# Attention in half-blocks of queries, ten hidden tiles in the first FFN, and the rows of the maxima sent from ScalarE's queue

## What is computed

```
x = x + attn(ln(x))      # 16 heads of 16, rotary, causal softmax over 1024 keys, output matrix Wo
x = x + ffn(ln(x))       # down(silu(gate(x)) * up(x)), hidden 768, weights int / 127
x = x + wkv(ln(x))       # RWKV-6 time mixing: five mixed inputs, decays, scan with a 64x64 state per head
x = x + ffn(ln(x))       # the same weights
```

## Time and profile before

| | |
|---|---|
| median of 3 runs | 3494.27 us (3494.21 to 3497.56) |
| the profiled execution | 3494.36 us, of which the span from first to last instruction is 3492.6 |
| busy share of the span | PE 86%, VectorE 71%, ScalarE 37%, GpSimd 39% |
| mean granted TensorE clock | 0.943 of 2.4 GHz |
| one batch in the middle | 422 to 424 us from one batch's first maxima to the next's |

### The profile page before, as it was taken

How to read it: one execution, slowest core, us unless ns; L and a number is a source line. 1 busy time by engine, 2 the same in 40 slices (tenths; PEclk the granted TensorE clock), 3 DMA queues, 4 the chain that set the end, 5 groups by cost and what they waited for, 6 DMA issues and landing times.

```text
span 3492.6 us, 47078 instructions
## 1 busy us (share of the span) xinstructions
PE 3005.8 (86%) x17056; PEld 1832.7 (52%) x17056; DVE 2492.0 (71%) x5105; ACT 1308.3 (37%) x2721; POOL 1351.1 (39%) x1276
## 2 busy tenths in 40 slices
PE   2488988889888888889888898889988889898898
PEld 1236565365643666335663457535565355753667
DVE  4575787667875687857878568785687857877566
ACT  0264323632346322453225532265313643136322
POOL 0123561245612365124551346313462134622455
PEclk9699998999989999899998999999998999989999
DMA  3600024000330005100150002400024000240000
GB/s 129 111 2 13 19 37 81 2 13 19 59 59 2 13 19 79 39 14 10 22 92 15 14 10 43 83 2 13 15 40 81 2 14 19 37 80 2 1 1 13
DMA packets 68888, 115.04 MB, mean 33 GB/s; under 512 B 10796, under 2 KB 64076, under 8 KB 65532
## 3 DMA queue, kind: packets, MB, share of 16 engines
q1 hardware_dynamic: 68627, 111.51, 16.1%
HBM read 74.69 MB, written 33.65 MB: 31 GB/s over the span
## 4 chain that ended last, share of the span: by engine, by line
PE 47%; DVE 29%; POOL 11%; issue 4%; ACT 4%; DMA 2%; SPq 0%; DVEq 0%; POOLq 0%; ACTq 0%
DVE mxp L989 9%; PE PB L1342 7%; PE PB L1327 5%; PE PB L1417 5%; PE PB L1313 5%; PE PB L1402 4%; DVE arena L1182 4%; PE PB L1456 3%; PE PB L1375 3%; DVE attn L911 3%; DVE arena L1191 2%; PE PB L1491 2%; ACT arena L744 2%; PE PB L1481 2%; POOL hl L607 2%
## 5 line engine op out<-in xcount | busy, mean ns | idle before, releaser
L989 DVE TENSOR_REDUCE mxp<-PB 128x1 f32<-128x512 f32 (+3 forms) x1536 | 755.3, 549 | 165.8 <-PE PB L1313 93.4
L744 ACT ACTIVATE arena<-PB 128x512 f32<-128x512 f32 (+3 forms) x1536 | 653.9, 507 | 460.3 <-PE PB L1327 453.4
L1313 PE MATMUL PB<-arena 96*128 96x512 bf16 (+3 forms) x1536 | 522.1, 368 | 104.4 <-DVE mxp L989 62.4
L597 POOL TENSOR_SCALAR_AFFINE_SELECT arena<-arena 128x512 f32<-128x512 f32 x256 | 162.8, 636 | 1003.6 <-ACT arena L744 1003.3
L1327 PE MATMUL PB<-arena 99*128 99x512 bf16 (+3 forms) x1536 | 472.7, 347 | 25.6 <-DMA arena<-augT 18.4
L1313 PEld LDWEIGHTS PB<-arena 96*128 96x128 bf16 x1536 | 156.6, 103 | 429.7 <-DVE mxp L989 328.9
L607 POOL TENSOR_TENSOR hl<-arena,hh 128x512 fp32r<-128x512 f32 x192 | 251.7, 1311 | 263.3 <-ACT hh L769 259.3
L1342 PE MATMUL PB<-arena 128*32 128x512 f32 (+3 forms) x3072 | 340.1, 515 | 15.5 <-ACT attn L733 13.7
L1402 PE MATMUL PB<-xh,wgu 128*128 128x512 f32 x768 | 312.8, 407 | 20.9 <-DVE xres L972 8.6
L1402 PE MATMUL PB<-xl,wgu 128*128 128x512 f32 x768 | 305.7, 398 | 3.1 <-issue 3.1
L1586 PE MATMUL PB<-arena 128*128 128x128 f32 x1792 | 235.4, 283 | 56.1 <-DVE arena L1182 46.7
(11 more groups left out here) (141 smaller groups left out, 5397.7 us busy)
## 6 DMA issues: line engine op xcount, KB each, us to landing
arena<-parts SPq DMA_DIRECT2D x112, 256.0 KB, 9.7
parts<-arena SPq DMA_DIRECT2D x192, 128.0 KB
arena<-parts SPq DMA_DIRECT2D x16, 768.0 KB, 18.2
arena<-in_x SPq DMA_DIRECT2D x16, 512.0 KB, 4.4
arena<-parts SPq DMA_DIRECT2D x16, 512.0 KB, 20.5
xres<-in_x SPq DMA_DIRECT2D x16, 512.0 KB, 4.2
out<-xres SPq DMA_DIRECT2D x16, 512.0 KB, 13.9
wgu<-arena SPq DMA_DIRECT2D x2, 768.0 KB, 4.5
```

Source lines behind the costliest of these rows:

```text
L597: pool.affine_select(out=a, in_=a, compare_op=ALU.is_ge, fill=0.0, base=0, pattern=[[0, HG], [1, 128]], channel_multiplier=-1).then_inc(ma ...
L744: act.activation(pt[:, U % 3, h, 0:n], bank(b, "score", t)[:, 0:n], ACT.Exp, scale=DH ** -0.5).then_inc(act_emptied, 1)
L989: dve.reduce_max(mxp[:, g % 2, h, col:col + 1], bank(b, "max", g * NPC + k)[:, 0:n], axis=AX.X).then_inc(dve_emptied, 1)
L1313: last = mm(ps[:, 0:n], qst[0:AUG, h, 128 * i:128 * i + 128], kst[0:AUG, h, s0:s0 + n], start=True, stop=not diag)
```

## The change

Attention is planned by blocks k = 2g + f, a group's first or second half of queries. The layout of the stacks is turned so that a half is contiguous. The list of max items falls from 192 to 152 per batch: short diagonal pieces of two or four heads share a bank and are reduced by one VectorE instruction with an output of two or four columns (columns and matmuls stay as many). The step list is made by `score_steps`: block k's scores may start 15 steps after its last maxima, at 0.6 score items per step at first, and at 1.27 from step 52 on. Executed, the list gives 165 steps: 25 with maxima alone, 27 with 16 scores, 100 (52 to 151) with 125 scores, and 13 with the other 51 scores alone. The last max item of each block is in steps 10, 37, 48, 75, 86, 113, 124, 151, and its transposes in steps 15, 42, 53, 80, 91, 118, 129, 153.

The splitting of the maxima moves from VectorE (6 small instructions a group) to GpSimd (5 a block), with one join per group left on VectorE. One DMA per block on ScalarE's queue replaces three per group on SP's. `den` works by block, with three instructions: the wide copy is left out, and the second transpose reads a broadcast. Two of four output projections are issued three steps before the end of attention, the other two behind the first gate and up matmuls of the first FFN, whose second half of x comes at e = 4 (was 2) and whose first down matmuls at e = 8 (was 9). The first FFN's tiles move below word 16384, with 10 slots in place of 7. The second FFN keeps its places, 7 slots and orders. The other regions that overlapped (`x0`, the split tiles, `turned_late`) are moved.

```diff
 def score_units():
-    return [(j, f) for j in range(NT) for f in (0, 1) if 128 * j < HALF * (f + 1)]
+    return [(j, f) for f in (0, 1) for j in range(4 * f + 4)]
...
+    for f in (0, 1):
+        if f:
+            out.append([((h,), i, 0, HALF, i) for i in range(4, NT) for h in range(HG)])
+        else:
+            out.append([])
+        for a in (3, 2, 1, 0):
+            n = 128 * (a + 1)
+            heads = [(h,) for h in range(HG)] if a >= 2 else [(0, 1), (2, 3)] if a else [tuple(range(HG))]
+            out[f] += [(hs, 4 * f + a, HALF * f, n, 4 * f + a + 4 * f) for hs in heads]
...
-DOWN_AT = 6
-V_AT = (8, 20)
-SLOTS = 7
+DOWN_AT = {1: 4, 3: 6}
+SECOND_AT = {1: 4, 3: 2}
+V_AT = (4, 8)
+SLOTS = {1: 10, 3: 7}
...
-LAG = 12
-DELAY = NPC + LAG
-AUG_AT = 3
+LAG = 15
+AUG_AT = 5
+def score_steps():
+    done, credit, out = 0, 0.0, []
+    for t in range(NMAX):
+        ready = [k for k in range(2 * NG - 1) if t >= BLOCK_END[k] + LAG]
+        most = HG * (LAST_UNIT[ready[-1]] + 1) if ready else 0
+        credit = min(credit + (1.27 if t >= BLOCK_END[1] + LAG else 0.6), 2.0)
+        n = max(0, min(int(credit), most - done))
+        credit -= n
+        done += n
+        out.append(done)
+    while done < NSC:
+        done = min(NSC, HG * (done // HG + 1))
+        out.append(done)
+    return out
...
-        add(b, "o", range(3), "dve")
+            if t == O_STEP:
+                add(b, "o", (0, 1), "dve")
         add(b, "ln1", (0, 1), "dve")
-        add(b, "o", (3,), "dve")
...
+        ffn_sets = {1: ffn_tiles(1, 0, 4096 + 512 * TURNS), 3: ffn_tiles(3, HIGH, HIGH + 4096 + 512 * TURNS)}
...
-                    for g in range(NG):
-                        wait_emptied(sp, b, "aug", g)
-                        for r in range(3):
-                            sp.dma_start(qst[AUG + r:AUG + r + 1, HG * g:HG * g + HG, :],
-                                         augT[32 * r:32 * r + 32, g % 2, :]).then_inc(aug_loaded[g], 16)
...
+                        pool.tensor_scalar(parts_[0], m, -1.0, 1.0, ALU.mult, ALU.mult).then_inc(aug_chain, 1)
+                        pool.wait_ge(aug_chain, 40 * b + 5 * k + 1)
+                        pool.tensor_tensor(augf[:, :, :], m, parts_[0], ALU.add).then_inc(aug_chain, 1)
+                        pool.wait_ge(aug_chain, 40 * b + 5 * k + 2)
+                        pool.tensor_scalar(parts_[1], augf[:, :, :], -1.0, 1.0, ALU.mult, ALU.mult).then_inc(aug_chain, 1)
...
+                    for t in range(STEPS):
+                        if t in BLOCK_END:
+                            max_parts(BLOCK_END.index(t))
+                        for U in DIAG_UNITS:
+                            if UNIT_STEP[U] == t:
+                                mask_unit(U)
+                        if t in DEN_STEP:
+                            over_sums(DEN_STEP.index(t))
+                        if t == O_STEP:
+                            over_sums(2 * NG - 2)
                     ln_scale(1, b, 0)
-                    ln_scale(1, b, 1)
+                    over_sums(2 * NG - 1)
...
+                    def max_rows(k):
+                        wait_emptied(act, b, "aug", k)
+                        act.dma_start(qst[AUG:AUG + 3, k % 2, HG * (k // 2):HG * (k // 2) + HG, :],
+                                      augT[:, k % 2, :]).then_inc(aug_loaded[k], 16)
...
+                    def den(k):
+                        dve.transpose(sums, attn[:, 4 * f:4 * f + 4, g, :]).then_inc(den_chain, 1)
+                        dve.reciprocal(one, sumT[:, f, :].rearrange("p (a n) -> p a n", n=32)[:, :, DH:DH + 1]).then_inc(den_chain, 1)
+                        dve.transpose(sumT[:, f, :].rearrange("p (a n) -> p a n", n=32),
+                                      one.broadcast_to([128, HALF // 32, 32])).then_inc(den_chain, 1)
...
+                    residual("o", 0, 0)
+                    residual("o", 1, 0)
+                    ln_half(1, 0)
+                    den(2 * NG - 1)
+                    x_low(1, 0, (0, 1))
...
+                            if e == 1 and k == 1:
+                                dve.wait_ge(x_loaded[1], 16 * (b + 1))
+                                residual("o", 2, 0)
+                                residual("o", 3, 0)
+                                ln_means(1, b, 1, stats, mv)
+                            if e == 2 and k == 1:
+                                ln_norm(1, b, 1, xres, xn, mv, rstd)
...
+                        if t == O_STEP:
+                            out_proj(0)
+                            out_proj(1)
+                    pv(NG * len(UNITS) - 2)
+                    pv(NG * len(UNITS) - 1)
+                    transpose_x(1, (0, 1))
...
+                            if e == 1 and k == 1:
+                                out_proj(2)
+                                out_proj(3)
```

More of the change, by code:

```diff
@@ L82, in ffn @@
             for e in range(2 * NM):
-                if f == 0 and e == 4:
+                if f == 0 and k == 1 and e == 2:
+                    add(b, "o", (2, 3), "dve")
+                if f == 0 and e == 2 * SECOND_AT[k]:
                     add(b, f"ln{k}", (2, 3), "dve")
-                if f == 1 and e == DOWN_AT:
+                if f == 1 and e == DOWN_AT[k]:
                     add(b, f"dn{k}", (0, 1), "dve")
@@ L106, in ahead @@
                 add(nxt, kind, ns, who)
-        for t in range(NSC + DELAY):
-            if t < NSC:
+        for t in range(STEPS):
+            if t < NMAX:
                 add(b, "max", (t,), "dve")
@@ L112, in psum_plan @@
                 add(b, "v", (2 + V_AT.index(t),), "act")
[L113 to L116, removed]
-        add(b, "o", range(3), "dve")
+            if t in AUG_STEP:
+                add(b, "aug", (AUG_STEP.index(t),), "dve")
+            add(b, "score", scores_of(t), "act")
+            if t == O_STEP:
+                add(b, "o", (0, 1), "dve")
         add(b, "ln1", (0, 1), "dve")
-        add(b, "o", (3,), "dve")
         ffn(b, 1)
@@ L334, in build @@
         stacked = [sem(f"stacked{m}") for m in (0, 1)]
+        max_joined = sem("max_joined")
         aug_chain = sem("aug_chain")
-        aug_loaded = [sem(f"aug_loaded{g}") for g in range(NG)]
+        aug_loaded = [sem(f"aug_loaded{k}") for k in range(2 * NG)]
         masked = sem("masked")
@@ L611, in _ @@
                         h_low_part(1, 0, e)
-                        if e == 1 and ahead:
+                        if e == 0:
+                            ln_scale(1, b, 1)
+                        if e == 5 and ahead:
                             ln_scale(0, b + 1, 0)
@@ L740, in _ @@
                         n = HALF * (f + 1) - max(HALF * f, 128 * j)
+                        for k in range(2 * NG):
+                            if ROWS_AT[k] == t:
+                                max_rows(k)
                         wait_filled(act, b, "score", t)
@@ L757, in ffn @@
                     def ffn(k, s):
+                        xh, _, turn, hh, _ = ffn_sets[k]
                         def x_parts(ns):
@@ L1046, in _, with max_piece @@
-                    aug_out(NG - 1)
-                    for g in (NG - 2, NG - 1):
-                        for step in range(4):
-                            den(g, step)
+                    def max_piece(t):
+                        k, (hs, i, s0, n, col) = MAXES[t]
+                        wait_filled(dve, b, "max", t)
+                        dve.reduce_max(mxp[:, k // 2 % 2, hs[0]:hs[-1] + 1, col:col + 1],
+                                       bank(b, "max", t)[:, 0:n * len(hs)].rearrange("p (h n) -> p h n", n=n),
+                                       axis=AX.X).then_inc(dve_emptied, 1)
@@ L1051, in x_low @@
+                    for t in range(STEPS):
+                        if t < NMAX:
+                            max_piece(t)
+                        if t in BLOCK_END[1::2]:
+                            join_max(BLOCK_END.index(t) // 2)
+                        if t in AUG_STEP:
+                            aug_out(AUG_STEP.index(t))
+                        if t in DEN_STEP:
+                            den(DEN_STEP.index(t))
+                    den(2 * NG - 2)
                     def x_low(k, s, ns):
+                        xh, xl, _, _, _ = ffn_sets[k]
@@ L1096, in ffn @@
                                 low(b + 1, 1 + e)
-                            if e == 4 and k == 1 and ahead:
+                            if e == 6 and k == 1 and ahead:
                                 x0_norm(b + 1, 0)
@@ L1344, in pv, with out_proj @@
                         last.then_inc(pv_units, 1)
-                    for t in range(NSC + DELAY):
-                        if t in (0, 2 * NPC):
-                            pe.wait_ge(stacked[t // (2 * NPC)], 9 * 16 * (b + 1))
-                        if t < NSC:
-                            max_item(t // NPC, t % NPC)
+                    def out_proj(n):
+                        wait_bank(pe, b, "o", n)
```

(7 more changed lines are left out.)

339 lines of the change are left out of this document (154 added, 185 removed).

## The result

The changed kernel takes 3459.5 us (median of 4 runs, 3457.0 to 3464.6) against 3494.2 before: ratio 0.990, 95% interval 0.989 to 0.992. It is faster by 35 us, 4.3 a batch, where I had forecast 142, 17.7 a batch. The time lies outside my range of 3262 to 3440.

The account below looks back on a forecast made before the run. Attention's stages had different limits, the middle losing 6.5 us a group by coupling of evenly loaded PE and VectorE. Savings of 12.2 + 5.5 = 17.7 us a batch, 142 in eight, took 3494.4 to 3352 us; range 3262 to 3440.

Parts of the forecast that it names:

- The maxima before the first score: Start of a batch's attention: 60 steps become 25, taking 14.5 us in place of 29.8.
- Steps 25 to 51: Attention's thin lead of maxima with few scores: 17.5 us a batch, bounds 15.2 and 25, with a fall of the clock.
- rival (e): Clock stays low through steps 25 to 51 and 20 us more, costing all the gain: about 3492 us; chance 3%.
- The middle stage: Attention steps 52 to 151: a group takes 33 us in place of 35.0, 86 us a batch, bounds 75.5 and 99.
- rival (a): Attention's middle: the finer mix fills both engines, a group takes 29.5 us, 73 us less: 3279 us; chance 15%.
- Rival (b): Attention's maxima rows come late, eight waits a batch of 1 us each, 64 us more: 3416 us; chance 14%.
- The first is the ring of seven: First FFN: PE's 5.16 us wait for `hl` comes from seven hidden tiles; ten slots and earlier down matmuls save 5.5 us a batch.
- the tail: Attention's end, scores alone plus two output projections: 23.7 + 7.1 - 2.8 = 28.0 us, bounds 27 and 31.
- the first FFN's own work: First FFN: 41.1 us less 5.5 a batch, after allowing for residuals, statistics and norms moved onto VectorE there.
- The way to the first gate: Last product with v to first gate matmul: 13.0 us in place of 19.6, bounds 11 and 17; 13 was also a sign.
- Rival (c): First FFN gains nothing because VectorE with its moved work becomes the limit, 44 us more: 3396 us; chance 12%.
- On SP the queue only gets shorter: Rows' DMAs moved to ScalarE's queue: issue 0.59 us, 8 a batch, 4.7 us if uncovered; SP still reloads x as before.

Follow-up runs that it names:

- experiment 8: Changed kernel with the five small instructions of each block's maxima split moved from GpSimd back to VectorE: 3521.8 us, ratio 1.0090.
- experiment 3: Kernel before, ring still seven, with VectorE's norm for time mixing moved behind the gate of e = 11 in the first FFN: 3448.5 us, 0.9867.
- experiments 4 and 10: First FFN's ring set back to seven slots: in the changed kernel 3456.8 us (0.9896), in the kernel with the four orders mended 3348.1 us (0.9582).
- Experiment 1: Changed kernel with GpSimd's `over_sums` of the block before the last put ahead of the same step's triangle: 3425.6 us, 0.9803.
- experiment 9: The four orders mended, but with the next batch's statistics put back ahead of the gate of e = 5: 3372.3 us, 0.9647.
- experiment 7: Changed kernel with the eight DMAs of the rows issued from SP's queue, behind the reload of x: 3491.6 us, 0.9991.
- the four orders mended: Changed kernel, sums and power earlier on GpSimd, time-mixing norm behind gate e = 11, next batch's statistics behind gate e = 5 on VectorE: 3351.5 us, 0.9586.

## Why the prediction was wrong

**Right.** The direction. The maxima before the first score: 14.5 forecast, 14.5 measured. Steps 25 to 51: 17.5 forecast, 17.9 measured (987.6 to about 1005.5 us). The clock fell in the lead and came back soon after (0.70 over 987.6 to 1001.4, then 1.00), so rival (e) didn't happen.

**Nearly right.** The middle stage: 33 us a group forecast, 31 measured, with VectorE's 26.1 busy us where I had 26.8. That is the edge of my 31 to 35 and nearer to rival (a)'s 29.5; the loss by coupling fell from 6.5 us a group to 4.8, and which part of the new order did it was not tried. VectorE's work in this loop counts in full: experiment 8 prices 40 small instructions a batch at 62 us over the launch (the old kernel had 24 of them there). Rival (b) named the right kind of thing in the wrong place: the rows' chain costs PE 28.3 us of waits in the whole launch, in this batch mostly the 1.4 us at the first and the last block, and not 8 a batch.

**Wrong, first: "The first is the ring of seven".** This step gave 5.5 us a batch. The wait that it was to remove was made by the norm for time mixing ahead of the gate of e = 10 (experiment 3: 45.6 us in the old kernel, 5.7 a batch, with the ring and ScalarE's wait for it untouched). Seven tiles or ten make no difference in the changed kernel (experiments 4 and 10). In the old kernel the ring held ScalarE for 5.66 us, and the prediction took this for the cause: it went from a real wait in the code to PE's wait without asking VectorE's timeline what stood before the gate of e = 10. Since the norm kept its place in the change, the wait stayed (5.49 us) with its low clock.

**Wrong, second: the tail, 28.0 us, came out at 34.8,** outside its bounds of 27 to 31. The step that failed is the overlap: I added the projections' 7.1 us and let PE's idle time of 3.6 us take 2.8 of them. Instead PE's idle time rose to 5.6. I didn't follow `over_sums` on GpSimd's queue, where the change puts it behind a triangle that needs the exponents of the same step. Experiment 1 gives 4.2 of the 6.8 us: 3.57 of wait and 8.83 - 7.17 = 1.7 of clock make 5.2 in the trace's batch, 4.2 on the mean of all batches and runs. The rest of the tail's miss wasn't tried on its own; 1.46 us of wait for the last block's split stand in it.

**Wrong, third: the first FFN's own work.** I named the work moved to VectorE and the chain to the first gate matmul, but gave them no more than 3 us together. Without its two projections the first FFN takes 51.6 - 7.1 = 44.5 us, where it took 41.1 and I had 35.6. The way to the first gate was 6.5 us. My sign for it, 13, was wrong by its own change, since it counts two projections that now stand behind the first gate; without them it is 5.9. The low clock behind that gate and the wait of 2.37 for `hl` of e = 5 came on top. The places of power and statistics in their queues cost 23.5 and 20.8 us (experiment 9), 5.5 a batch. Rival (c), the FFN gains nothing, came true with a surplus of 3.4 us, though its reason, VectorE as the limit, is only half of it: what limits is the order on VectorE and GpSimd.

**Unpriced.** "On SP the queue only gets shorter" was true and beside the point. The lead of 14.5 us holds only with the rows on another queue: left on SP's they come later than the first score needs them, which costs 32 us (experiment 7), and the whole change is then worth 2. No run takes the rest of the change apart: the plan by blocks, the pieces that share a bank, the place of the projections.

With the four orders mended, which leave every instruction's work as it is, the kernel takes 3351.5 us, where I had put the forecast at 3352. That is luck and no merit of the sum: 31 us of it are the norm's place, which I had booked under the ring at 44, and the attention loop gave 3.7 us a batch more than forecast.

## What to carry to other kernels

A wait in the trace names the last instruction of a chain. So go up that engine's own timeline and ask what stood before it, and whether the thing before it was itself waiting; only then look into the code for a ring or a semaphore. When a change moves an instruction in a loop that several engines walk in step, write down for each engine what it now stands behind: four such places, of 21 to 34 us each, are worth 108 us here, three times the change itself. And where two engines are evenly loaded in a loop, small instructions put on one of them can count in full, and a small DMA behind a waiting one can cost as much as it waits.

## What was not expected of the hardware

A short wait of PE can cost more than its length. The 3.57 us before the projection were followed by a stretch at 0.57 in which 32 matmuls took 8.83 instead of 7.17 us. But waits of one length don't all end so. In front of the down matmuls at e = 8 PE waited 2.37 us for `hl` in the changed kernel and 2.37 us in experiment 9, and the windows behind these waits show a full clock in the first and the half one in the second:

```profile
1157.10:1158.10 1.00, 0.94 (x8) 0.97 (x9) 0.00 (x0) 0.00 (x0) 0.92 (x2) 1.00 0.00 0
...
1128.70:1129.70 1.00, 0.98 (x4) 1.00 (x5) 0.00 (x0) 0.00 (x0) 0.92 (x2) 0.50 0.00 0
```

What decides wasn't tried. Under the projection's matmuls the clock came back, 0.54 over 1110 to 1112 us and 1.00 over 1112 to 1114. The Trainium skill ("TensorE: Matmul & The Clock Gate", "Part 1: The HAM clock gate") says that activity releases the throttle; both levels here are its two, and the trace agrees. And a DMA's issue took 0.73 us on ScalarE's queue, where the earlier trace rows had 0.59 on SP's: the view of one line's instructions in the changed kernel, ns min/median/max.

```profile
L811 ACTq DMA_DIRECT2D arena<-augT x64: 728/729/1350, 130.1 to 3184.0; - x64
```
